# One base for eight tiles of edges and 80 accumulator columns, in place of four tiles and 64 columns, in a graph network of 200,000 edges

## The chip, the cores and the metric

The kernel runs on one core of one Trainium2 chip. The metric is the device time of one execution in microseconds (us); the median of three runs is the time that counts. TensorE is the matmul engine, VectorE and ScalarE the elementwise engines, GpSimd (POOL in the profile) issues the indirect gathers, SyncE (SP) issues plain DMAs.

## What is computed

Four graph layers stand one behind the other, each ahead of it with a layer norm and a residual. Nodes: 12500, with 128 features each. Edges: 200,000, as pairs (src, dst), sorted by dst, so that the edges of one node are neighbours; a node has 16 edges in the mean. All is float32.

```python
def sage(x, src, dst, W, b):                      # layer 0, three times
    agg = segment_sum(x[src], dst, n) * inv[:, None]
    return relu(concatenate([x, agg], -1) @ W + b)

# layer 1: attention over the edges of a node (4 heads of 32), then a feed-forward block
msg = xh[src] * alpha[:, :, None]
out = segment_sum(msg, dst, n)                    # and the sum of alpha beside it

# layer 2: msg = relu(h[src] + edge_attr); aggr = segment_sum(msg, dst, n); two batch norms
# layer 3: x + segment_sum(x[src] + edge_attr, dst, n)
```

What takes the time is `segment_sum(x[src], dst)`: a gather of 200,000 rows of 512 bytes and a sum by sorted destination.

## The kernel before

**Tiles, groups, halves, iterations.** Edges are padded to 98 × 16 tiles of 128 (`TILE`). A tile's rows are gathered into SBUF, one edge in a partition. `GT` = 4 tiles are a group, and 16 tiles (`HALF`) are a half; `GPH` = 16 / `GT` = 4 groups are in a half, `NGRP` = 392 in all. An iteration does two halves, h = 0 and 1; there are `NIT` = 49 iterations.

**The sum by one-hot matmuls.** For each group the smallest dst is its base. `rel_n` holds dst minus base for each edge. VectorE compares it with 0 .. `W` - 1 (`W` = 64) and gets a one-hot matrix of 128 × W for each tile (L803, 16 tiles in one instruction). TensorE multiplies gathered rows and one-hot (L751), and the tiles of a group accumulate in one PSUM bank (`bank_of`), 128 features × W nodes. VectorE then adds the bank to the transposed result `A` at column base (L846); the base is read from SBUF into a register first (L837). If a group spanned W nodes or more, `net.rounds` would be over 1 and the walk would be made again with the window moved by W.

**Stages.** `aggregate` is called six times: agg0, agg1, agg2 (layer 0), agg3 (attention), agg4 (layer 2, `edges`), agg5 (layer 3).

- agg0 also counts edges for each node: VectorE folds the one-hots of a group by L811, and TensorE sums them over the partitions by L756.
- agg0, agg1, agg2 and agg5 are *dense*: as soon as a stretch of 500 nodes is complete (`due`), its dense layer is computed within the same loop, in banks 4 to 7. Their groups have `NB` = 4 banks, the others 8.
- agg3 gathers nothing: its rows were gathered before by `gat_gather` (L1191) and come by plain DMA. A second matmul with 4 weight columns sums the attention weights (L765, 128*4).
- agg4 adds the edge features (loaded by SyncE, L715 to L728) to the rows (L831, VectorE) and applies ScalarE's relu (L661). A second matmul (L765, 128*128) sums the edge features themselves, for agg5. Its edges are dealt to partitions so that a partition's edge features of one group are contiguous: `GT` × 512 bytes.

**Who waits for whom.** Gathers for half h of iteration i + 1 go into the buffer of half h of iteration i, so GpSimd waits for `summed[h]`, which TensorE raises by one for each group (L677); in agg4 it waits for VectorE's `message[h]` (L675). Ahead of each group TensorE waits for `added` (L748), that the add of the group that had the bank is done. VectorE's order in an iteration is written out: stage the index of the next iteration (L162), adds of half 0, compare for half 0 of the next iteration, in agg4 its message too, adds of half 1, dense chunks if due, compare for half 1.

Of the kernel before, what the change touches and what calls it, by code (L numbers as in the profile page):

```python
# [18 lines left out]
I32 = mybir.dt.int32  # L19
# [5 lines left out]
E = 200000  # L25
D = 128
P = 128
# [3 lines left out]
NSUB = N // SUB  # L31
TILE = 128
HALF = 16
GT = 4
GPH = HALF // GT
NHALF = 98
NIT = NHALF // 2
NTILE = NHALF * HALF
NGRP = NTILE // GT
EP = NTILE * TILE  # L40
GE = GT * TILE
W = 64
EPP = EP // P
H = 4
C = D // H
# [53 lines left out]
def allocate(net):  # L99
# [3 lines left out]
    net.work = net.sb("work", [P, 2 * HALF * XW])  # L103
    net.onehot = net.sb("onehot", [P, 2, HALF, W])
    net.src_n = net.sb("src_n", [P, NTILE + 2 * HALF])
# [218 lines left out]
def prepare(net):  # L324
# [6 lines left out]
    nc = net.nc  # L331
    GP = NGRP // GPH
# [7 lines left out]
    src_i = net.B[0:GP, 0:GPH * GE].bitcast(I32)  # L340
    src_f = net.B[0:GP, 2048:2048 + GPH * GE]
    dealt = [net.B[:, 4096 + k * NTILE:4096 + (k + 1) * NTILE] for k in range(2)]
    least, most = net.small[0:GP, 0:GPH], net.small[0:GP, 4:8]
    span = net.small[0:GP, 8:9]
    least_i = net.small[0:GP, 12:16].bitcast(I32)
    row = net.small[0:1, 16:20]
    it_i = net.work[:, 0:W].bitcast(I32)
    zeros = net.C[:, 0:2 * H * NSC // P // 2]
# [3 lines left out]
    lists = [(src_f, net.src_n, False), (rel_f, net.rel_n, False), (src_f, dealt[0], True), (rel_f, dealt[1], True)]  # L352
    tiles = [(fr, to, deal, g, k) for fr, to, deal in lists for g in range(GPH) for k in range(GT)]

    with nc.Block() as block:
# [34 lines left out]
        def _(dve):  # L390
# [59 lines left out]
            for n, (_, to, _, g, k) in enumerate(tiles):  # L450
                dve.wait_ge(turned, n + 1)
                nc.vector.tensor_copy(to[:, 0:NTILE].rearrange("p (a t) -> p a t", t=HALF)[:, :, g * GT + k],
                                      net.psum[:, (n % 2 + 2) * 512:(n % 2 + 2) * 512 + GP]
# [3 lines left out]
        def _(pe):  # L457
# [4 lines left out]
            for n, (fr, _, deal, g, k) in enumerate(tiles):  # L462
                if n >= 2:
                    pe.wait_ge(copied, n - 1)
                group = fr[:, g * GE:(g + 1) * GE]
                tile = (group.rearrange("a (p k) -> a k p", k=GT)[:, k, :] if deal
                        else group[:, k * TILE:(k + 1) * TILE])
# [128 lines left out]
def aggregate(net, tag, table=None, extra=None, follow=None):  # L596
# [10 lines left out]
    nc = net.nc  # L607
# [20 lines left out]

    high = [P, H if attention else P]
    dense = follow and follow.dense  # L630
    NB = 4 if dense else 8
    bank_of = lambda h, q, k: net.psum[0:high[k], (h * SG + q) % NB * 512 + k * W:(h * SG + q) % NB * 512 + (k + 1) * W]
    name = lambda k: [net.sem(f"{tag}_{k}{h}") for h in range(S)]
    index_ready = net.sem(f"{tag}_index")
# [3 lines left out]
    message, attr_loaded, relued = name("message"), name("attr"), name("relued")  # L638
# [6 lines left out]
    with nc.Block() as block:  # L645
# [40 lines left out]
        @block.sync  # L686
        def _(sp):
            if not (attention or edges):
                if dense:
                    follow.sync(sp)  # L690
                return
            if edges:
                sp.dma_start(net.src_n[:, 0:NTILE], net.DEALT[0]).then_inc(lists, 16)
                sp.dma_start(net.rel_n[:, :], net.DEALT[1]).then_inc(lists, 16)
                sp.wait_ge(cleared, 1)
            R = sp.value_load(net.rounds[0:1, 0:1], min_val=1, max_val=256)
            with sp.Fori(0, R) as r:
                with sp.Fori(0, NIT) as i:
                    n = sp.snap(r * NIT + i)
                    for h in range(2):  # L700
                        if attention:

                            sp.wait_ge(message[h], n + 1)
                            sp.dma_start(rows[h], net.G[bass.ds(i * 2 + h, 1), :, :]
                                         .rearrange("a p f -> (a p) f")).then_inc(gathered[h], 16)
                        else:

                            sp.wait_ge(summed[h], n * GPH + GPH)  # L710
                            lane = "(q p k) f -> p q (k f)"
                            slots = attr[h].rearrange("p (q f) -> p q f", q=GPH)
                            edge = net.dram["edge_attr_128"]
                            at = (2 * i + h) * HALF * TILE
                            sp.dma_start(slots[:, 0:2, :], edge[bass.ds(at, 2 * GE), :].rearrange(  # L715
                                lane, q=2, p=P)).then_inc(attr_loaded[h], 16)
                            if h == 0:
                                sp.dma_start(slots[:, 2:4, :], edge[bass.ds(at + 2 * GE, 2 * GE), :].rearrange(
                                    lane, q=2, p=P)).then_inc(attr_loaded[h], 16)
                                continue  # L720
                            with sp.If(i < NIT - 1):
                                more = nc.s_assert_within(at + 2 * GE, 0, E - 2 * GE)
                                sp.dma_start(slots[:, 2:4, :], edge[bass.ds(more, 2 * GE), :].rearrange(
                                    lane, q=2, p=P)).then_inc(attr_loaded[h], 16)
                            with sp.Else():
                                rest = E - (NGRP - 2) * GE
                                sp.dma_start(slots[0:rest // GT, 2, :], edge[E - rest:E, :].rearrange(
                                    "(p k) f -> p (k f)", k=GT)).then_inc(attr_loaded[h], 16)  # L728

        @block.tensor  # L730
# [154 lines left out]
class Shares:  # L885

    dense = False
# [12 lines left out]
class Sage:  # L900
# [6 lines left out]
    dense = True  # L907
# [113 lines left out]
class Project:  # L1021
# [6 lines left out]
    dense = True  # L1028
# [807 lines left out]
class Finish:  # L1836


    dense = True
# [100 lines left out]
```

## Time and profile before

| What | us |
|---|---|
| Runs, median of three (lowest, highest) | 16836.19 (16834.64, 16855.76) |
| Profiled execution, its own time | 16957.4 |
| Profiled execution, span from first to last instruction | 16955.6 |
| GpSimd busy | 9653.8 (57%) |
| TensorE busy, matmul | 6756.4 (40%) |
| VectorE busy | 3233.9 (19%) |
| ScalarE busy | 824.7 (5%) |

The mean granted clock of TensorE is 0.528 of full speed (2.4 GHz), so over most of the span it is the lower of its two levels, 1.2 GHz. Busy shares are means over stages that differ: what an edit is worth is read from its stage. In the rows, POOL is GpSimd, DVE is VectorE, PE is TensorE's matmul and PEld its weight load; L680 is line 680 of the kernel. Idle time stands in brackets in front of the instruction that ends it, with what released it as the profile infers; "remote" and "issue" mean that it names no instruction of this core.

### The profile page before, as it was taken

What the parts mean: (1) busy time and instruction counts of PE and PEld (TensorE: products, weight loads), DVE (VectorE), ACT (ScalarE), POOL (GpSimd) and SP (SyncE); (2) the same over time, 40 slices, a digit from 0 to 9 for tenths busy, and PEclk for the clock granted to TensorE, in tenths of its full rate; (3) what the DMA queues carried; (4) which work ended last, traced back from release to release, by engine and by line L of the source; (5) the groups of instructions that cost most, each with busy time, mean ns of one, the idle gap of its engine ahead of it and who ended that gap; (6) DMA issues with size and microseconds to landing.
All of it is one profiled execution on the core that took longest, in us unless ns stands there. A gap on an engine that the chain in (4) does not pass through costs nothing. (4 is left out here: it accounts for less than half of the span.)

```text
span 16955.6 us, 119259 instructions
## 1 busy us (share of the span) xinstructions
PE 6756.4 (40%) x30243; PEld 5863.6 (35%) x30244; DVE 3233.9 (19%) x6147; ACT 824.7 (5%) x1247; POOL 9653.8 (57%) x9860
## 2 busy tenths in 40 slices
PE   3444443333334444410000009995555555533333
PEld 2333333333333333300000008873555554333333
DVE  3222221000011212200000014444111112311111
ACT  1000000000000000000000000003000000200000
POOL 2666666666666666667777440002666664366666
PEclk8555555555555555555555555557555555655555
DMA  2111111111111221233333212222222222221212
GB/s 87 47 48 47 48 48 45 48 48 48 48 47 53 55 55 54 57 87 100 100 100 99 66 33 87 97 89 84 82 81 80 82 82 89 67 54 52 54 53 53
DMA packets 593155, 1124.64 MB, mean 66 GB/s; under 512 B 220825, under 2 KB 364384, under 8 KB 566578
## 3 DMA queue, kind: packets, MB, share of 16 engines
q0 software_dynamic: 307488, 624.42, 14.6%
q1 hardware_dynamic: 285622, 499.73, 8.8%
q8 instruction: 15, 0.25, 0.0%
q14 instruction: 30, 0.25, 0.0%
HBM read 904.32 MB, written 218.95 MB: 66 GB/s over the span
## 5 line engine op out<-in xcount | busy, mean ns | idle before, releaser
L680 POOL DMA_INDIRECT work<-rows_a,index x4704 | 4587.5, 975 | 2399.1 <-issue 1544.6
L751 PE MATMUL psum<-onehot,work 128*128 128x64 f32 x12544 | 2822.4, 419 | 4459.8 <-DMA work<-rows_a,index 2818.1
L751 PEld LDWEIGHTS psum<-onehot,work 128*128 128x128 f32 x12544 | 2717.3, 328 | 4556.2 <-issue 4424.5
L680 POOL DMA_INDIRECT work<-rows_b,index x3136 | 3118.6, 994 | 1771.6 <-issue 1075.8
L1191 POOL DMA_INDIRECT work<-attention_rows,index x1568 | 1610.9, 1027 | 612.5 <-issue 557.2
L751 PE MATMUL psum<-onehot,regionB 128*128 128x64 f32 x6272 | 1551.9, 416 | 720.1 <-issue 581.2
L751 PEld LDWEIGHTS psum<-onehot,regionB 128*128 128x128 f32 x6272 | 1440.3, 327 | 819.6 <-issue 801.5
L846 DVE TENSOR_TENSOR regionA<-regionA,psum 128x64 f32 x2352 | 508.0, 216 | 5289.9 <-remote 2271.8
L765 PE MATMUL psum<-onehot,regionB 128*4 128x64 f32 (+1 forms) x6272 | 1174.7, 358 | 484.9 <-issue 484.5
L765 PEld LDWEIGHTS psum<-onehot,regionB 128*4 128x4 f32 (+1 forms) x6272 | 1023.8, 223 | 533.3 <-issue 486.8
L182 POOL COPY work<-regionB 128x500 f32 (+1 forms) x75 | 45.5, 606 | 2034.9 <-DVE regionB L561 2034.9
L843 DVE TENSOR_TENSOR regionC<-regionC,psum 128x64 f32 (+1 forms) x1176 | 254.1, 216 | 3594.7 <-remote 2155.8
L1339 PE MATMUL psum<-ident,work 128*128 128x128 f32 x49 | 17.6, 454 | 2214.4 <-POOL work L1294 2214.2
L1339 PEld LDWEIGHTS psum<-ident,work 128*128 128x128 f32 x49 | 8.9, 182 | 2223.1 <-POOL work L1294 2221.4
L803 DVE TENSOR_TENSOR onehot<-rel_n,window 128x1024 f32<-128x1024 f32 x588 | 717.9, 1221 | 244.7 <-issue 225.0
L162 DVE CAST index<-src_n (+1 forms) x301 | 56.0, 187 | 2180.3 <-DMA work<-attention_rows,index 2073.4
L831 DVE TENSOR_TENSOR regionB<-work,regionB 128x2048 f32<-128x2048 f32 x98 | 225.1, 2297 | 449.7 <-DMA regionB<-in_edge_attr 290.0
L661 ACT ACTIVATE regionB<-regionB 128x2048 f32<-128x2048 f32 x98 | 187.2, 1910 | 2402.9 <-DVE regionB L831 1896.4
L756 PE MATMUL psum<-regionC,ones 128*128 128x64 f32 x784 | 246.4, 409 | 88.4 <-issue 87.6
L969 PE MATMUL psum<-regionB,weights 128*128 x100 | 101.5, 1118 | 445.8 <-DVE regionA L959 356.2
L984 ACT ACTIVATE turn<-psum,small 128x500 f32<-128x500 f32 x50 | 33.9, 678 | 4498.1 <-PE psum L970 3033.5
L756 PEld LDWEIGHTS psum<-regionC,ones 128*128 128x128 f32 x784 | 214.2, 328 | 77.7 <-issue 77.7
(253 smaller groups left out, 4471.5 us busy)
## 6 DMA issues: line engine op xcount, KB each, us to landing
gathered_rows<-work SPq DMA_DIRECT2D x98, 1088.0 KB
work<-gathered_rows SPq DMA_DIRECT2D x98, 1088.0 KB, 4.9
regionB<-in_edge_attr SPq DMA_DIRECT2D x195, 512.0 KB
work<-rows_a,index POOLq DMA_INDIRECT x4704
work<-rows_b,index POOLq DMA_INDIRECT x3136
work<-attention_rows,index POOLq DMA_INDIRECT x1568
x_transposed<-regionA SPq DMA_DIRECT2D x75, 250.0 KB, 6.0
rows_a<-regionC SPq DMA_DIRECT2D x50, 250.0 KB
```

What stands on the lines that cost most here:

```text
L162: return net.nc.vector.tensor_copy(net.index[:, :, :].rearrange("p a t -> p (a t)")[:, bass.ds(parity * 2 * HALF, 2 * HALF)], net.src_n[:, ...
L661: nc.scalar.activation(msgs[h], msgs[h], ACT.Relu).then_inc(relued[h], 1)
L680: pool.indirect_dma_start(rows3[h][:, t, :], None, table, bass.IndirectOffsetOnAxis(ap=net.index[:, k, h * ST + t:h * ST + t + 1], axis=0) ...
L751: last = nc.tensor.matmul(bank_of(h, q, 0), msgs3[h][:, t, 0:D], onehot[:, h * ST + t, :], start=(k == 0), stop=(k == GT - 1))
L756: last = nc.tensor.matmul(bank_of(h, q, 1), net.ones[:, :], piles[h][:, q * W:(q + 1) * W], start=True, stop=True)
L765: last = nc.tensor.matmul(bank_of(h, q, 1), lhs, onehot[:, h * ST + t, :], start=(k == 0), stop=(k == GT - 1))
L803: nc.vector.tensor_tensor(onehot[:, h * ST:(h + 1) * ST, :], net.rel_n[:, bass.ds(i * 2 * HALF + h * ST, ST)].unsqueeze(2) .broadcast_to([ ...
L831: nc.vector.tensor_tensor(msgs[h], rows[h], attr[h], ALU.add).then_inc(message[h], 1)
L843: nc.vector.tensor_tensor(Cc[0:high[1], bass.ds(at, W)], Cc[0:high[1], bass.ds(at, W)], bank_of(h, q, 1), ALU.add)
L846: nc.vector.tensor_tensor(A[:, bass.ds(at, W)], A[:, bass.ds(at, W)], bank_of(h, q, 0), ALU.add).then_inc(added, 1)
L969: net.nc.tensor.matmul(dense(net, 0), self.w[:, 0:D], net.col(net.B, c), start=True, stop=False)
L1191: pool.indirect_dma_start(rows3[h][:, t, :], None, net.XH, bass.IndirectOffsetOnAxis(ap=net.index[:, k, h * HALF + t:h * HALF + t + 1], ax ...
```

## The change

A group has eight tiles (1024 edges) in place of four, and its accumulator 80 columns in place of 64. So there are two groups in a half and 196 in all. Everything derived from `GT` and `W` follows: the one-hots are 128 × 80 for each tile, 128x1280 in one compare; a group's matmuls accumulate eight tiles; each half has two reports, two value loads of a base and two adds (of 80 columns) in place of four. The number of edge matmuls stays. `NB` becomes 2 × `GPH` = 4 in all stages; that is an iteration's groups. In agg4 a half's edge features are loaded by one DMA for each group, of the same 512 KB, with contiguous pieces of 4 KB in place of 2 KB.

```diff
-GT = 4
+GT = 8
-W = 64
+W = 80
-    least, most = net.small[0:GP, 0:GPH], net.small[0:GP, 4:8]
+    least, most = net.small[0:GP, 0:GPH], net.small[0:GP, 4:4 + GPH]
-    least_i = net.small[0:GP, 12:16].bitcast(I32)
+    least_i = net.small[0:GP, 12:12 + GPH].bitcast(I32)
-    NB = 4 if dense else 8
+    NB = 2 * GPH
-                            lane = "(q p k) f -> p q (k f)"
-                            sp.dma_start(slots[:, 0:2, :], edge[bass.ds(at, 2 * GE), :].rearrange(
-                                lane, q=2, p=P)).then_inc(attr_loaded[h], 16)
+                            sp.dma_start(slots[:, 0, :], edge[bass.ds(at, GE), :].rearrange(
+                                "(p k) f -> p (k f)", p=P)).then_inc(attr_loaded[h], 16)
                             if h == 0:
-                                sp.dma_start(slots[:, 2:4, :], edge[bass.ds(at + 2 * GE, 2 * GE), :].rearrange(
-                                    lane, q=2, p=P)).then_inc(attr_loaded[h], 16)
+                                sp.dma_start(slots[:, 1, :], edge[bass.ds(at + GE, GE), :].rearrange(
+                                    "(p k) f -> p (k f)", p=P)).then_inc(attr_loaded[h], 16)
...
-                                rest = E - (NGRP - 2) * GE
-                                sp.dma_start(slots[0:rest // GT, 2, :], edge[E - rest:E, :].rearrange(
+                                rest = E - (NGRP - 1) * GE
+                                sp.dma_start(slots[0:rest // GT, 1, :], edge[E - rest:E, :].rearrange(
```

## Rows read from the trace of the kernel before

**Rows 1.** GpSimd's busy time and its gather lines; durations as minimum/median/maximum in ns.
```profile
PE 6756.4 (40%) x30243; PEld 5863.6 (35%) x30244; DVE 3233.9 (19%) x6147; ACT 824.7 (5%) x1247; POOL 9653.8 (57%) x9860
...
L680 POOL DMA_INDIRECT work<-rows_a,index x4704 | 4587.5, 975 | 2399.1 <-issue 1544.6
...
L1191 POOL DMA_INDIRECT work<-attention_rows,index x1568 | 1610.9, 1027 | 612.5 <-issue 557.2
...
L680 POOL DMA_INDIRECT work<-rows_a,index x4704: 942/947/1997, 291.9 to 16930.3; - x196
```

**Rows 2.** Length; PE, PEld, DVE, ACT, POOL busy; clock: agg1, agg3, agg4.
```profile
2620.60:4940.60 2320.00, 814.15 (x3340) 723.28 (x3340) 246.99 (x584) 45.80 (x75) 1536.76 (x1581) 0.51 0.18 48
...
...
10255.20:11370.20 1115.00, 1115.00 (x6265) 984.16 (x6266) 543.32 (x1097) 0.00 (x0) 0.00 (x0) 0.50 0.27 96
11759.40:14279.20 2519.80, 1386.87 (x6138) 1370.42 (x6138) 494.47 (x1009) 185.25 (x97) 1594.10 (x1568) 0.50 0.28 81
```

**Rows 3.** Waits of GpSimd's gathers: total us, times, longest.
```profile
POOL work L680 <- remote: 996.8, 188, 6.7
...
POOL work L680 <- DVE regionB L831: 433.5, 32, 18.2
```

**Rows 4.** Timeline within agg1: start us, length us, engine, line, count, idle time before.
```profile
3992.83 7.09 PE L751 MATMUL psum<-onehot,work 128*128 128x64 f32 x32 [19.37 <-DMA work<-rows_b,index]
...
4006.53 0.22 DVE L846 TENSOR_TENSOR regionA<-regionA,psum 128x64 f32 x1 [11.26 <-remote]
...
4015.71 0.22 DVE L846 TENSOR_TENSOR regionA<-regionA,psum 128x64 f32 x1 [8.96 <-remote]
4016.39 0.95 POOL L680 DMA_INDIRECT work<-rows_b,index  x1 [5.25 <-remote]
4016.72 0.22 DVE L846 TENSOR_TENSOR regionA<-regionA,psum 128x64 f32 x1 [0.79 <-DVE regionA L846]
4017.06 1.23 DVE L803 TENSOR_TENSOR onehot<-rel_n,window 128x1024 f32<-128x1024 f32 x1
4017.65 1.46 POOL L680 DMA_INDIRECT work<-rows_b,index  x1 [0.30 <-issue]
```

**Rows 5.** VectorE's compare, count reduce and message: busy us, mean ns of one.
```profile
L803 DVE TENSOR_TENSOR onehot<-rel_n,window 128x1024 f32<-128x1024 f32 x588 | 717.9, 1221 | 244.7 <-issue 225.0 <-DVE base_now L792 2.9
...
L831 DVE TENSOR_TENSOR regionB<-work,regionB 128x2048 f32<-128x2048 f32 x98 | 225.1, 2297 | 449.7 <-DMA regionB<-in_edge_attr 290.0 <-DMA work<-rows_b,index 151.7 <-issue 8.0
...
L811 DVE TENSOR_REDUCE regionC<-onehot 128x256 f32<-128x1024 f32 x98 | 186.3, 1901 | 3.5 <-issue 0.2
```

**Rows 6.** Timeline within agg1: three transposes of 128 moving columns.
```profile
4028.96 0.84 PE L1001 MATMUL psum<-ident,turn 128*125 128x128 f32 x3
```

**Rows 7.** Timeline within agg3: TensorE's groups, large and small matmuls in turn.
```profile
10604.39 1.02 PE L765 MATMUL psum<-onehot,regionB 128*4 128x64 f32 x8
...
10605.33 1.97 PE L751 MATMUL psum<-onehot,regionB 128*128 128x64 f32 x8
...
10607.23 0.38 PE L765 MATMUL psum<-onehot,regionB 128*4 128x64 f32 x2
```

**Rows 8.** Timeline within agg4: single matmuls, then the end of a pause.
```profile
13081.93 0.27 PE L765 MATMUL psum<-onehot,regionB 128*128 128x64 f32 x1 [2.53 <-issue]
...
13083.33 0.27 PE L765 MATMUL psum<-onehot,regionB 128*128 128x64 f32 x1 [1.14 <-issue]
...
13085.63 0.22 DVE L843 TENSOR_TENSOR regionC<-regionC,psum 128x64 f32 x1 [34.04 <-remote]
...
13086.10 0.39 SPq L715 DMA_DIRECT2D regionB<-in_edge_attr  x1
...
13088.34 1.23 DVE L803 TENSOR_TENSOR onehot<-rel_n,window 128x1024 f32<-128x1024 f32 x1
...
13091.34 2.29 DVE L831 TENSOR_TENSOR regionB<-work,regionB 128x2048 f32<-128x2048 f32 x1 [1.77 <-DMA regionB<-in_edge_attr]
...
13094.45 0.95 POOL L680 DMA_INDIRECT work<-rows_b,index  x1 [14.90 <-DVE regionB L831]
```

More of the change, by code:

```diff
@@ L714, in _ @@
                             at = (2 * i + h) * HALF * TILE
-                            sp.dma_start(slots[:, 0:2, :], edge[bass.ds(at, 2 * GE), :].rearrange(
-                                lane, q=2, p=P)).then_inc(attr_loaded[h], 16)
+                            sp.dma_start(slots[:, 0, :], edge[bass.ds(at, GE), :].rearrange(
+                                "(p k) f -> p (k f)", p=P)).then_inc(attr_loaded[h], 16)
                             if h == 0:
-                                sp.dma_start(slots[:, 2:4, :], edge[bass.ds(at + 2 * GE, 2 * GE), :].rearrange(
-                                    lane, q=2, p=P)).then_inc(attr_loaded[h], 16)
+                                sp.dma_start(slots[:, 1, :], edge[bass.ds(at + GE, GE), :].rearrange(
+                                    "(p k) f -> p (k f)", p=P)).then_inc(attr_loaded[h], 16)
                                 continue
                             with sp.If(i < NIT - 1):
-                                more = nc.s_assert_within(at + 2 * GE, 0, E - 2 * GE)
-                                sp.dma_start(slots[:, 2:4, :], edge[bass.ds(more, 2 * GE), :].rearrange(
-                                    lane, q=2, p=P)).then_inc(attr_loaded[h], 16)
+                                more = nc.s_assert_within(at + GE, 0, E - GE)
+                                sp.dma_start(slots[:, 1, :], edge[bass.ds(more, GE), :].rearrange(
+                                    "(p k) f -> p (k f)", p=P)).then_inc(attr_loaded[h], 16)
                             with sp.Else():
-                                rest = E - (NGRP - 2) * GE
-                                sp.dma_start(slots[0:rest // GT, 2, :], edge[E - rest:E, :].rearrange(
+                                rest = E - (NGRP - 1) * GE
+                                sp.dma_start(slots[0:rest // GT, 1, :], edge[E - rest:E, :].rearrange(
                                     "(p k) f -> p (k f)", k=GT)).then_inc(attr_loaded[h], 16)
```

## The prediction

> **What bounds the kernel now.** I read the page first. GpSimd is busy 57% of the span, no engine more, and nearly all of it is gathers, one indirect DMA for 128 edges: 7840 of L680 and 1568 of L1191 [rows 1]. Then the stretches of the stages that walk over the edges, three of which stand in [rows 2]. In those that gather, GpSimd is by far the busiest engine or (agg4) level with TensorE; TensorE is busy all the time in one alone, the attention sum (10255 to 11370), which gathers nothing. So two bounds: the GpSimd chain in agg0, agg1, agg2, agg4 and agg5, TensorE in agg3.
>
> The timeline of one iteration of agg1 shows how the GpSimd chain is built [rows 4]. A gather takes 0.95 us and the next starts 0.30 us behind it, 1.25 us each, so 32 gathers are 40.0 us. An iteration takes 2320.0 / 49 = 47.3 us [rows 2], the start of the stage included (46.5 in the steady part). The difference has two parts. One is a pause of 5.25 us ahead of the gather at 4016.39: it refills the buffer of half 0 and must wait until TensorE has reported the last group of that half (`summed[0]`). The whole run has 188 such waits, 996.8 us [rows 3]. The report is late, not the matmuls: half 0's 32 matmuls are recorded from 3992.83 to 3999.92, yet VectorE adds its second group at 4006.53 and its third at 4015.71, 4 to 5 us after GpSimd stopped. I don't know what holds the reports back; I only see that they come through when the gathers stop. The other part is collisions: the gather that starts at 4017.65, under VectorE's one-hot compare, takes 1.46 us and not 0.95. All gathers of that kind together have a median of 947 ns and a mean of 975 [rows 1]: 28 ns × 1568 = 44 us in each stage, 0.45 us for each of its 98 compares.
>
> **The change part by part.**
>
> Matmuls, 64 to 80 columns. In steady state a 128x128 matmul of 64 columns takes (7.09 - 0.42) / 31 = 0.215 us, the last one's recorded 0.42 us aside [rows 4]. One of 128 columns takes (0.84 - 0.42) / 2 = 0.21 us at the same clock [rows 6]. The pace is therefore set by something that 64 and 128 columns share (both load 125 or 128 weight columns), and 80 lies between them: 0. This covers L751, L756 and the edge matmuls of L765. Not so the attention's small matmuls with 4 weight columns: eight of them with 64 columns take 1.02 us, a pace of about 0.107 [rows 7], and by columns it becomes 0.133. A group of four tiles in agg3 takes 10607.23 - 10604.39 = 2.84 us: 8 × 0.107 for the small ones, 8 × 0.2135 for the large ones, and 0.28 for the two changes between the shapes. Two old groups are 5.69 us. A new group of eight tiles is 16 × 0.2135 + 16 × 0.133 + 0.28 = 5.83. So +0.14 us × 196 groups = **+27 us**, all on the path, as TensorE never rests there. Ends: +84 if the changes of shape cost nothing less often (3136 × 0.027), -55 if the small ones don't grow at all (196 × 0.28).
>
> Compare, L803, from 1024 to 1280 elements. 1024 take 1.22 us and 2048 (L831, the same kind of instruction) 2.30 [rows 5], 1.05 ns an element: 1.49 us, +0.27. VectorE has room for it (247 of 2320 us busy in agg1 [rows 2]), so by itself it costs nothing; through the gathers it does. A gather that starts during a compare ends about 0.81 us after the compare's end: 4017.65 + 1.46 is 0.82 after 4018.29 [rows 4]. It is held until the compare is over. A compare that is 0.27 longer thus holds GpSimd 0.27 longer where it already held it, and the row of the mean says that nearly every compare does. That is the lower end: 0.27 × 98 × 4 = 106 us in the four gathering stages beside agg4, 92 if one compare in eight falls where no gather is due.
>
> The add, L846, from four groups in a half to two. Two of four adds go; each takes 0.22 us and starts 0.8 to 1.0 us behind the one before it, and the compare stands behind the last. What the adds give back is VectorE time that nobody waits for. But the compare moves. Before, the late report let VectorE add the third group at 4015.71, the fourth at 4016.72 and compare at 4017.06. Now the last group's add is the one at 4015.71; the compare runs from 4016.05 to 4017.54. GpSimd restarts at 4016.39 as before, and its first gather is held: to 4017.54 + 0.81 = 18.35, 1.96 us and not 0.95 (the longest gather of before took 1997 ns [rows 1]). The second one is free of it. So +1.01 - 0.51 = +0.50 us, 0.23 more than from the length alone. The compare of half 1 also comes earlier, at random against the gathers: between +0.27 and +0.50. Upper end: 1.0 us × 49 × 4 = 196 us. Between 92 and 196 I take **+125 us**, since in agg0 and agg2 the work after the adds (reduce, dense chunk) already shifts the compare away from the restart.
>
> The Trainium skill, "SBUF — State Buffer", section "Who interferes with whom", says that a VectorE instruction with two SBUF inputs contends with a GpSimd instruction that reads SBUF, and that whoever is second waits for the whole instruction; one with a PSUM input doesn't count. By that rule the adds taken away give the gathers nothing and the compare made longer costs them all of its length; the trace agrees (1.46 us under L803, 0.95 under the L846 at 4016.72).
>
> Counts in agg0. The reduce L811 (1.90 us for 1024 elements [rows 5]) grows to about 2.4 us 98 times, the count matmul halves. The reduce stands behind the compare, TensorE needs it some 20 us later: 0. If it held gathers as the compare does, +0.47 × 98 = +46 us.
>
> Banks and waits. With two groups in a half, four banks hold two halves, so in dense stages a matmul no longer waits for the add of the half before. That wait fell on half 1, whose result GpSimd wants some 20 us later: 0. Nothing is queued behind new waits.
>
> The edge stage, agg4. Its pauses are longer: 433.5 us until L831 [rows 3]. In the one shown, VectorE gets the reports at 13085.63, adds groups 1.12 us apart, compares at 13088.34 and then still waits 1.77 us for the edge load that was issued at 13086.10; L831 starts at 13091.34 and GpSimd 3.1 us later [rows 8]. Adds saved (2 × 1.1) and compare grown (0.27) both vanish behind the load. The load moves the same bytes with half as many pieces, 4 KB instead of 2 KB; no row has a 4 KB piece. It took 13091.34 - 13086.10 = 5.2 us; I bound it between nothing and 1 us less, 0 to -49 us, and set it against the compares that hold gathers here (0.27 × 98 = +26): **0**, ends -50 and +60.
>
> Preparation: 64 transposes and copies as before, bases in one row of 196: 0. SyncE's and ACT's queues issue what they did.
>
> The pause itself. TensorE runs the same matmuls in each half; only its reports are half as many. I keep the pause at its length; what speaks against that is a rival.
>
> Sum: 27 + 125 + 0 = +152 us. The profiled execution goes from a span of 16955.6 (16957.4 with what lies around it) to 17109. The median of the runs is 0.7% below it; the same sum on it gives 16836 + 152 = **16988 us**, say 16990.
>
> **The rivals.**
>
> Faster: the pause shrinks. The reports come through one at a time while gathers run (second group 4006.53, third 4015.71, that is 9 to 11 us apart), and half as many might all be through before GpSimd needs the last one. For: those distances. Against: in agg4, while gathers run, single matmuls follow each other 1.4 us apart (13081.93, 13083.33), the engine idle 2.53 and 1.14 us ahead of them [rows 8], so the price looks like one for each matmul, and these stay as many; and the third and fourth group are added 1.0 us apart, so they are let through together when gathers stop. Price: 996.8 us of pauses; half gone is -500, with +152 it gives 16490. It decides from 0.8 us off each of the 188 pauses (152 / 188), from where the sum turns negative.
>
> No change: what the compare takes from a gather is given back by the pause, since the pause ends at a fixed moment of TensorE and not so long after the last gather. Then only agg3 is left, 16863. For: the pause is a wait. Against: the reports are released by GpSimd's stopping.
>
> Slower, more: with sixteen matmuls to a report the first one is late as well, and VectorE gets both at the restart; pauses grow by 1 us: +196 + 152, 17185.
>
> The change doesn't do what it says: if eight tiles spanned 80 nodes anywhere, `rounds` would be 2 and each aggregation would run twice, about 29,000 us. The drawn destinations span at most 71 in any 1024 edges, 37 in any 512, so one round in both.
>
> **How the numbers follow.** Forecast 0.57 (all slower); pause shrinks 0.24 (nearly all faster, the smallest gains within 0.2%); given back 0.12 (within 0.2%, which is 34 us and about what a measurement can tell from no change); pause grows 0.06; two rounds 0.01. Faster 0.23, same 0.14, slower 0.63. The likeliest case alone runs from 16836 + 92 - 55 - 50 = 16823 to 16836 + 196 + 84 + 60 + 46 = 17222. The range reaches down to a pause shortened by somewhat over two fifths, 16550, and up to 17230.
>
> **What would show it.** L803 at 1.49 us, x588; L846 x1176. L680 with a mean near 990 and not 975, a median still 947. TensorE's L751 at the same mean of 419. agg3 27 us longer. The 188 waits at 5.3 us each. If their sum falls below 850 us, my step on the pause is wrong and the kernel is faster; if L680's mean stays, the step on the held gather is.

## The result and the profile after

The kernel with eight tiles to a group and 80 columns takes **16440.10 us** (median of 4 runs, 16433.56 to 16445.67) beside 16840.03 us of the kernel before on the same chip (16834.64 to 16855.76). The ratio is 0.977, 95% interval 0.9758 to 0.9782: 400 us faster, where 150 us slower was forecast, and below the range of 16550 to 17230. Unchanged on another chip it gave 0.9744 (0.9728 to 0.976).

The profiled execution spans 16443.0 us. Lines of the page, groups and the wait that answer to [rows 1], [rows 5] and [rows 3] (line numbers of the kernel after are one lower from L751 on):

```profile
PE 6230.6 (38%) x29851; PEld 5397.4 (33%) x29852; DVE 3125.4 (19%) x4383; ACT 824.4 (5%) x1247; POOL 9777.0 (59%) x9860
...
PEclk8555555555555555555555556986555556655555
```

```profile
L680 POOL DMA_INDIRECT work<-rows_a,index x4704 | 4663.9, 991 | 2270.4 <-issue 1540.1
L802 DVE TENSOR_TENSOR onehot<-rel_n,window 128x1280 f32<-128x1280 f32 x588 | 874.9, 1488 | 226.7 <-issue 216.1 <-DVE base_now L791 3.0
```
```profile
L845 DVE TENSOR_TENSOR regionA<-regionA,psum 128x80 f32 x1176 | 273.2, 232 | 5257.0 <-remote 2816.2 <-PE psum L750 1408.5 <-DMA running_max<-regionC 700.6
```
```profile
POOL work L680 <- remote: 737.9, 150, 6.2
```

GpSimd is busy longer, not shorter (9777 us, before 9654): its gathers still collide, and more. The digit row is the news: TensorE's granted clock, 5 tenths in most of the run, shows 6, 9 and 8 where agg3 lies. The windows of agg1, agg3 and agg4 (length, busy time of PE, PEld, DVE, ACT, POOL, clock, DMA share, GB/s) say how much that is, against [rows 2]:

```profile
2618.30:4902.30 2284.00, 814.12 (x3336) 725.22 (x3336) 221.33 (x374) 45.73 (x75) 1556.61 (x1569) 0.51 0.18 48
10205.00:10959.20 754.20, 678.34 (x6272) 627.13 (x6272) 511.37 (x705) 0.00 (x0) 0.00 (x0) 0.90 0.40 142
11343.90:13781.80 2437.90, 1394.64 (x6098) 1354.91 (x6098) 456.22 (x623) 183.32 (x96) 1611.02 (x1568) 0.50 0.28 83
```

agg3, the one stage that TensorE bounds, fell from 1116 us at a clock of 0.50 to 754 us at 0.90: 362 of the 400 us. The timeline of its start shows the level change (start, length, engine, line, count; the trace holds two records for each matmul, so x16 is eight tiles and the x8 of [rows 7] four, and what the prediction counts as 32 matmuls of a half are the records of 16):

```profile
10204.95 3.70 PE L750 MATMUL psum<-onehot,regionB 128*128 128x80 f32 x16 [12.04 <-DVE regionB L824]
10208.58 2.30 PE L764 MATMUL psum<-onehot,regionB 128*4 128x80 f32 x16
10210.81 3.70 PE L750 MATMUL psum<-onehot,regionB 128*128 128x80 f32 x16
10214.44 2.06 PE L764 MATMUL psum<-onehot,regionB 128*4 128x80 f32 x16
10216.44 2.01 PE L750 MATMUL psum<-onehot,regionB 128*128 128x80 f32 x16
10218.38 1.27 PE L764 MATMUL psum<-onehot,regionB 128*4 128x80 f32 x16
10219.58 2.01 PE L750 MATMUL psum<-onehot,regionB 128*128 128x80 f32 x16
```

At 1.2 GHz a group takes 10210.81 - 10204.95 = 5.86 us, within 0.03 of the 5.83 that was forecast. From 10216.44 on, at 2.4 GHz, it takes 3.14 us (10216.44 to 10219.58). 196 groups of 3.14 are 615 us; the rest of the 754 is 76 us in which TensorE waits (754.2 - 678.3) and 63 us that the groups at the low level take beyond 3.14 each. The waits are 24 of about 3.1 us, for VectorE's L824 (such as the one that ends at 10244.92), and each of the 24 later stretches at the low level begins during one or shortly behind it; with the first stretch they last 144 us.

### The profile page after: what moved, and what is told of

The parts are those of the page before. It is cut to its first block and busy times, and to the rows that moved or that the text cites. A ratio compares the mean times of both kernels' runs of the same rounds, so it can differ in the third digit from the quotient of the medians.

```text
span 16443.0 us, 107327 instructions
## 1 busy us (share of the span) xinstructions
PE 6230.6 (38%) x29851; PEld 5397.4 (33%) x29852; DVE 3125.4 (19%) x4383; ACT 824.4 (5%) x1247; POOL 9777.0 (59%) x9860
## 5 line engine op out<-in xcount | busy, mean ns | idle before, releaser
L680 POOL DMA_INDIRECT work<-rows_a,index x4704 | 4663.9, 991 | 2270.4 <-issue 1540.1
L750 PE MATMUL psum<-onehot,work 128*128 128x80 f32 x12544 | 2762.0, 418 | 4410.6 <-DMA work<-rows_a,index 3032.2
L680 POOL DMA_INDIRECT work<-rows_b,index x3136 | 3167.2, 1010 | 1618.4 <-issue 1073.4
L750 PE MATMUL psum<-onehot,regionB 128*128 128x80 f32 x6272 | 1177.6, 353 | 730.9 <-issue 462.0
L750 PEld LDWEIGHTS psum<-onehot,regionB 128*128 128x128 f32 x6272 | 1112.0, 267 | 790.7 <-issue 751.8
L845 DVE TENSOR_TENSOR regionA<-regionA,psum 128x80 f32 x1176 | 273.2, 232 | 5257.0 <-remote 2816.2
L764 PE MATMUL psum<-onehot,regionB 128*4 128x80 f32 (+1 forms) x6272 | 1024.1, 329 | 461.6 <-issue 461.3
L764 PEld LDWEIGHTS psum<-onehot,regionB 128*4 128x4 f32 (+1 forms) x6272 | 946.3, 210 | 493.0 <-issue 474.5
L802 DVE TENSOR_TENSOR onehot<-rel_n,window 128x1280 f32<-128x1280 f32 x588 | 874.9, 1488 | 226.7 <-issue 216.1
L842 DVE TENSOR_TENSOR regionC<-regionC,psum 128x80 f32 (+1 forms) x588 | 136.4, 232 | 3172.0 <-remote 2103.0
L810 DVE TENSOR_REDUCE regionC<-onehot 128x160 f32<-128x1280 f32 x98 | 225.2, 2298 | 3.3
```

The costliest lines, as they stand in the source:

```text
L680: pool.indirect_dma_start(rows3[h][:, t, :], None, table, bass.IndirectOffsetOnAxis(ap=net.index[:, k, h * ST + t:h * ST + t + 1], axis=0) ...
L750: last = nc.tensor.matmul(bank_of(h, q, 0), msgs3[h][:, t, 0:D], onehot[:, h * ST + t, :], start=(k == 0), stop=(k == GT - 1))
L764: last = nc.tensor.matmul(bank_of(h, q, 1), lhs, onehot[:, h * ST + t, :], start=(k == 0), stop=(k == GT - 1))
L802: nc.vector.tensor_tensor(onehot[:, h * ST:(h + 1) * ST, :], net.rel_n[:, bass.ds(i * 2 * HALF + h * ST, ST)].unsqueeze(2) .broadcast_to([ ...
L810: nc.vector.tensor_reduce(piles[h].rearrange("p (q w) -> p q w", w=W), onehot[:, h * ST:(h + 1) * ST, :].rearrange("p (q k) w -> p q w k", ...
L842: nc.vector.tensor_tensor(Cc[0:high[1], bass.ds(at, W)], Cc[0:high[1], bass.ds(at, W)], bank_of(h, q, 1), ALU.add)
```

## The experiments

Times of the runs on agg3, each against the kernel before on its own chip at its own time, and agg3 in each profile. "Tiles in a row" is how many tiles' matmuls of one shape (128 or 4 weight columns) follow each other on TensorE in agg3.

| kernel | tiles in a row, columns | time | ratio (95%) | agg3, clock |
|---|---|---|---|---|
| before, again | 4, 64 | 16834.8 | 1.0003 (0.9993-1.0014) | 1116.0, 0.50 |
| gt4_halfreports | 4, 64 | 16828.3 | 1.0000 (0.9987-1.0014) | 1116.0, 0.50 |
| gt4_w72 | 4, 72 | 16885.0 | 1.0028 (1.0016-1.0040) | 1163.0, 0.50 |
| after_runs8 | 4, 80 | 16913.2 | 1.0045 (1.0028-1.0062) | 1210.0, 0.50 |
| gt8_w64 | 8, 64 | 16727.9 | 0.9942 (0.9920-0.9965) | 1059.8, 0.50 |
| gt4_w72_runs16 | 8, 72 | 16584.0 | 0.9852 (0.9835-0.9869) | 844.2, 0.88 |
| gt8_w72 | 8, 72 | 16444.8 | 0.9771 (0.9749-0.9792) | 773.4, 0.85 |
| after | 8, 80 | 16440.1 | 0.9770 (0.9758-0.9782) | 754.2, 0.90 |
| gt4_w64_runs32 | 16, 64 | 16839.7 | 0.9951 (0.9935-0.9966) | 1023.1, 0.73 |
| gt8_w72_runs32 | 16, 72 | 16639.4 | 0.9834 (0.9816-0.9852) | 872.9, 0.81 |

### Which part of the change brings the clock

**gt8_w64**: eight tiles, 64 columns as before. Edges that lie 64 or more above their group's base are left out of the sums, and one round is forced (in `...`).

```
-W = 80
+W = 64
...
```


> The changed kernel with the window taken back from 80 to 64 columns, one round forced: edges whose destination lies 64 or more above their group's base are left out of the sums. Theory A (columns): what lets TensorE run at 2.4 GHz in the attention sum agg3 is the wider moving operand; with 64 columns the clock stays at 1.2 GHz there, agg3 takes 1090 to 1116 us as before, and the whole is about 16440 + 340 = 16780 us, less some 60 for shorter compares, 16720. Theory B (groups): it is the longer runs of one shape (16 and 16 matmuls in place of 8 and 8); then agg3 stays near 750 us and the whole is 16340 to 16400. On the pauses: if they shrank because of fewer reports and adds, the waits of GpSimd's gathers stay at or below 740 us in total; the collisions fall back from a mean gather of 0.99 to 0.975 us.

**gt8_w72**: `W = 72` in the kernel after. The widest group spans 71, so nothing is left out.

> The changed kernel with 72 columns in place of 80 (the widest group spans 71 nodes above its base, so that nothing is left out). Theory A (columns): the clock of agg3 is between: either as high as with 80 (agg3 near 750 us, the whole 16400) or as low as before (agg3 near 1110, the whole 16750). Theory B (groups): agg3 near 750 us, the whole 16400 us. In both the compare is 1.36 us and the mean gather 0.983.

**gt4_w72**: `W = 72` in the kernel before.

> The kernel before with 72 columns in place of 64, still four tiles in a group. Theory A (columns): if 72 are enough, the clock of agg3 rises here too, agg3 near 750 to 800 us and the whole about 16500; Theory B (groups): agg3 stays at 1.2 GHz and takes 1116 + 3136 x 0.013 = 1157 us, the whole is 16840 + 41 + about 60 for longer compares = 16940 us. The pauses stay at 188 and 1000 us.

**gt4_halfreports**: the kernel before, with one report of TensorE for two groups.

```
-                            last.then_inc(summed[h], 1)
+                            if q % 2:
+                                last.then_inc(summed[h], 2)
```


> The kernel before, but TensorE reports two groups at once (a semaphore increment of 2 behind every second group); matmuls, adds, banks and compares stay. If the number of reports sets the pauses, GpSimd's waits fall from 997 us to the 738 us of the changed kernel or below, and the whole to about 16600; if it is the adds, or the banks that a matmul waits for, they stay at 950 to 1050 us and the whole within 50 us of 16840. agg3's clock should stay low.

Their windows of agg3, in this order without the last:

```profile
10184.00:11243.80 1059.80, 1059.75 (x6272) 994.15 (x6272) 481.17 (x705) 0.00 (x0) 0.00 (x0) 0.50 0.29 101
```
```profile
10205.80:10979.20 773.40, 696.32 (x6272) 648.55 (x6272) 495.04 (x705) 0.00 (x0) 0.00 (x0) 0.85 0.39 138
```
```profile
10215.30:11378.30 1163.00, 1162.96 (x6272) 1016.19 (x6272) 562.75 (x1097) 0.00 (x0) 0.00 (x0) 0.50 0.26 92
```

Neither part alone brings the clock. Both give my low-level terms back: eight tiles alone -56 us (I had 196 × 0.28 = 55), eight more columns alone +47 (3136 × 0.0133 = 42). TensorE is busy all of the 1060 and 1163 us, and still at 1.2 GHz. Reports half as many leave the time as it was (1.000). GpSimd's remote waits at L680 fell to 788.9 us in 175, which neither answer had (738 or less, or 950 to 1050); before_again, the unchanged kernel, has 888.8 in 175. Whatever its label, idle time over 1.5 us between gathers is 1112 us in agg0, agg1, agg2 and agg5 together, where three profiles of the unchanged kernel have 1158 to 1232. So fewer reports may shorten the pauses somewhat, but the half that my faster rival priced at 500 us does not go, and the kernel gains nothing.

**gt4_w72_runs16** and **after_runs8** change the order on TensorE in agg3: the one gives the kernel of four tiles (72 columns) the run length of eight tiles, the other gives the kernel after the run length of four. The first reports two groups at once; in the second the small sums also get banks of their own (not shown below).

```
+                            if attention:
+                                if q % 2 == 0:
+                                    continue
+                                for b, cols in ((0, slice(0, D)), (1, slice(D, D + H))):
+                                    for t in range((q - 1) * GT, (q + 1) * GT):
+                                        last = nc.tensor.matmul(bank_of(h, t // GT, b), ...)
+                                last.then_inc(summed[h], 2)
+                                continue
```
```
+                            if attention:
+                                for k0 in range(0, GT, 4):
+                                    for b, cols in ((0, slice(0, D)), (1, slice(D, D + H))):
+                                        for k in range(k0, k0 + 4):
+                                            last = nc.tensor.matmul(...)
+                                last.then_inc(summed[h], 1)
+                                continue
```


> Four tiles to a group and 72 columns, and in agg3 alone the order on TensorE is changed: the 16 matmuls of 128 rows... of 128 columns of weights for two groups and then the 16 of 4 columns for both, where it was 8 and 8 (one report for both groups). Theory A (the clock is granted by how long runs of one kind of matmul are, or by how densely TensorE streams without a change of shape): agg3 rises to 2.4 GHz as in the eight-tile kernels, takes 760 to 850 us in place of 1163, and the kernel 16480 to 16560. Theory B (the run length is not it; what eight tiles bring is something else, as fewer banks opened or fewer reads by VectorE): the clock stays at 0.50, agg3 takes 1163 less 49 to 60 for the shape changes saved, about 1108, and the kernel comes out near 16830.

> The kernel after (eight tiles, 80 columns), with the order of four tiles on TensorE in agg3 alone: 8 large... four large matmuls, four small, four large, four small, in one group's accumulators (the small ones in a bank of their own), so that shapes change as often as in the kernel before. Theory A (run length decides the clock): agg3 falls back to 1.2 GHz, takes about 1116 + 84 = 1200 us where it took 754, and the kernel takes 16440 + 445 = 16885, slower than before. Theory B (the run length is not it): the clock stays near 0.90, agg3 takes 754 plus some 30 for the shape changes at the high level, and the kernel 16470.

Windows of agg3, the first and then the second:

```profile
10214.80:11059.00 844.20, 678.17 (x6272) 629.60 (x6272) 562.29 (x1095) 0.00 (x0) 0.00 (x0) 0.88 0.36 127
```
```profile
10209.80:11419.80 1210.00, 1210.00 (x6272) 1042.32 (x6272) 515.57 (x705) 0.00 (x0) 0.00 (x0) 0.50 0.25 88
```

Theory A holds in both directions. The kernel after, with its matmuls in fours, loses the high clock and the whole gain (1210 us in agg3, 1.0045); the four-tile kernel in eights gets it (0.88; 844 us lie within the 760 to 850 expected, the kernel's 16584 is 24 above its range). What is left between 844 and 754 is waiting: TensorE is idle for 844.2 - 678.2 = 166 us, mostly for VectorE's adds, of which there are twice as many.

**gt4_w64_runs32** and **gt8_w72_runs32**: the same edit with all 16 tiles of a half in a row (`if q < SG - 1: continue`, `range(0, SG * GT)`), in the kernel before and in the kernel after with 72 columns.

> The kernel before (four tiles, 64 columns), with one change in agg3 on TensorE: the large matmuls of all 16 tiles of a half-iteration, then the small ones of all 16, reported together; so runs of one kind are four times as long as in before and twice as long as in the kernel of eight tiles and 64 columns, which stayed at a granted clock of 0.50. Theory A (only the length of the runs counts, and 64 columns need a longer run than 72 do): agg3 rises to 2.4 GHz, takes 760 to 860 us, and the kernel 16500 to 16590. Theory B (64 columns never get the high level in this pattern, however long the run; the accumulator's width is the second condition by itself): the clock stays at 0.50, agg3 takes 1116 less 1.5 times 56 or 1032, plus what TensorE now waits for the adds, and the kernel 16750 to 16830.

> Eight tiles and 72 columns, with agg3's large matmuls of both groups of a half-iteration first (16 tiles) and then the small ones of 16 tiles. The same kernel in runs of 8 tiles took 773 us in agg3 at a mean clock of 0.85, with single stretches at the low level in between. Theory A (a longer run holds the high level more firmly): the mean clock rises to 0.93 or more, agg3 takes 720 to 755 us and the kernel 16390 to 16430. Theory B (the level drops whenever TensorE has waited, and a report for 16 tiles at once makes it wait for VectorE's adds, as the four-tile kernel in runs of 8 tiles waited 178 us there): agg3 takes 780 to 860 us and the kernel 16450 to 16530.

```profile
10250.00:11273.10 1023.10, 782.18 (x6272) 755.38 (x6272) 546.45 (x1091) 0.00 (x0) 0.00 (x0) 0.73 0.30 105
```
```profile
10248.40:11121.30 872.90, 728.04 (x6272) 701.15 (x6272) 496.81 (x703) 0.00 (x0) 0.00 (x0) 0.81 0.35 123
```

The first falls between my two theories: 64 columns do reach the high level when the run is 16 tiles long, so 72 is no condition by itself, but only for part of the time, and one report for 16 tiles leaves TensorE idle for 241 us. The second goes theory B's way, somewhat past its 860 us: the mean clock falls from 0.85 to 0.81, TensorE waits 145 us where it waited 77, and the kernel is slower than with runs of eight. Both the run of one shape and the columns thus bear on the clock, as kernels compared here; why they do stays open. A longer run is no gain once a report comes too late for VectorE.

### The collisions, and what gives them back

**after_window_psum** and, unchanged, **window_psum_again**: the kernel after, with the compare's list of column numbers in PSUM in all aggregations but agg2.

```
+    window = net.window[:, :] if isinstance(follow, Project) else net.psum[:, 5 * 512:5 * 512 + W]
...
-            nc.vector.tensor_copy(net.window[:, :], net.window0[:, :])
+            nc.vector.tensor_copy(window, net.window0[:, :])
...
-                        net.window[:, :].unsqueeze(1).broadcast_to([P, ST, W]),
+                        window.unsqueeze(1).broadcast_to([P, ST, W]),
```


> The kernel after, with the list of column numbers that the comparison reads (the window) held in PSUM in every aggregation but the third, so that the comparison reads one operand from SBUF in place of two. In the kernel after a gather that begins under the comparison takes 1.46 us in place of 0.95, and the gathers of the dense stages carry 292 us more than at 0.945 us each, 292 against 224 at 64 columns. Theory A (the gathers suffer from the comparison's two SBUF inputs, and what they lose is on the path): the gathers' excess falls by 60 to 150 us over agg0, agg1 and agg5, and the kernel by 60 to 120, to 16320 to 16380. Theory B (the excess falls, but the pauses before the gathers grow by most of it, since both end with the same messages; as from 80 to 64 columns, where 68 us less excess came with 50 us more pauses): the kernel takes 16400 to 16440. Theory C (the length of the comparison alone counts, not where its operands lie): nothing moves, or reading PSUM makes the comparison slower than 1.49 us and the kernel 16450.

**before_again** and **before_third** are the kernel before, and **after_again** the kernel after, unchanged.

> The kernel before, unchanged, for a second profiled execution: the first one spans 16956 us, some 115 above the median of its runs, and its agg2 took 2341 us where three other four-tile kernels took 2277 to 2326. If that excess lies in single pauses of that one execution, this profile spans 16840 to 16900, its ratio is 1.000, agg3 takes 1116 us at a granted clock of 0.50 again, and agg4 comes out near 2486 as in the two other four-tile kernels, so that about 35 us of the 82 that agg4 seemed to lose by the change are the first profile's own. If the excess belongs to the kernel, agg2 is 2341 and agg4 2520 again.

> The kernel before, unchanged, as a partner for the runs beside it. In the last two experiments the kernel before took 15479 us on that occasion, where it had taken 16770 to 16950 on all others, and the traces taken there show hardly any waits of GpSimd for a late report. Theory A (the late reports come from outside the kernel and are there or not for a whole occasion): this profile has either some 170 to 190 such waits and 890 to 1000 us of them, with a time near 16840, or next to none, with a time near 15480, and nothing in between. Theory B (the two last experiments themselves took the waits away and the time of 15479 has another reason): the waits stand in this profile whatever its time.

> The kernel after, unchanged. With late reports: ratio 0.977 again, as collisions are given back by shorter pauses. Without late reports there is no pause that could give them back, and the sum of the prediction without its wrong step should hold: agg3 -362, collisions +92 to +125 over agg0, agg1, agg2 and agg5, so 15479 - 250 = about 15230, ratio 0.984 (0.982 to 0.986). The rival is that collisions cost nothing there either: 15479 - 362 = 15117, ratio 0.977.

> The kernel after with the window in PSUM in all aggregations but the third, unchanged from its first run. With late reports: the time of the kernel after, within 0.1%, as before. Without late reports the collisions it takes away are on the path: it is faster than the kernel after by 150 to 230 us (the excess of the gathers, 226 us in the three stages), so near 15030, ratio 0.970. The rival (a gather's excess doesn't count) gives the time of the kernel after in either case.

after_window_psum took 16519.5 us (0.9767, 0.9747 to 0.9786), before_again 16834.8 (1.0003). before_third, after_again and window_psum_again ran on one chip: 16908.9 (1.0006), 16488.5 (0.9744) and 16503.3 us (0.9752, 0.9736 to 0.9768). Over agg0, agg1, agg2 and agg5 I added up, from each trace, what the gathers take beyond 0.945 us each, and the pauses over 1.5 us between them:

| agg0 + agg1 + agg2 + agg5 | before_third | after_again | window_psum_again |
|---|---|---|---|
| gathers beyond 0.945 us | 170 | 302 | 94 |
| pauses over 1.5 us | 1201 | 1065 | 1248 |
| time of the four stages | 9135 | 9148 | 9109 |

Gather lines and GpSimd's waits of after_again and then of window_psum_again:

```profile
L680 POOL DMA_INDIRECT work<-rows_a,index x4704 | 4674.1, 994 | 2287.7 <-issue 1538.0 <-remote 560.9 <-DMA running_max<-regionC 113.0
...
POOL work L680 <- remote: 787.8, 153, 6.6
```
```profile
L681 POOL DMA_INDIRECT work<-rows_a,index x4704 | 4533.1, 964 | 2402.8 <-issue 1552.9 <-remote 730.2 <-PE psum L751 58.6
...
L803 DVE TENSOR_TENSOR onehot<-rel_n,psum 128x1280 f32<-128x1280 f32 x490 | 726.0, 1482 | 175.8 <-issue 164.8 <-DVE base_now L792 2.9
...
POOL work L681 <- remote: 1017.4, 184, 7.0
```

The collisions are real: the change adds 132 us of them (agg0 45, agg1 33, agg2 28, agg5 26; the first profiles of the two kernels differ by 108), and a compare that reads one operand from PSUM, as long as the other (1482 ns against 1489), takes 208 us away. Neither moves the four stages' time by more than 0.5%: the pauses take 136 us less in the one case and 183 us more in the other. In agg0 of after_window_psum the starts of the halves are most often 20.0 and 26.1 us apart, 46.1 together; in before_again most often 20.4 and 25.7, and 46.1 or 46.2 together in 28 of 48 iterations. It is no constant: the medians of unchanged kernels lie between 46.0 and 46.7, and in agg1 of the kernel after the iterations spread evenly over 44.6 to 48.0. Theory B holds. The Trainium skill, "SBUF — State Buffer", section "Who interferes with whom", says that a VectorE instruction with at most one SBUF input, outside the modes that use two ports, does not contend with GpSimd; the traces agree (gathers at 964 ns in place of 994, and only in the stages so changed).

**after_halfrows**: in agg0, agg1, agg2 and agg5 each gather fetches 64 numbers in place of 128, and the buffer is cleared first. **after_halfmatmuls** and, unchanged, **halfmatmuls_again**: in those stages the scatter matmul of every second tile is left out.

```
-                            for k in range(GT):
+                            step = 1 if attention or edges else 2
+                            for k in range(0, GT, step):
```


> The kernel after, but in agg0, agg1, agg2 and agg5 each gather fetches 64 of the 128 numbers of a row (as many rows, half the bytes; what is computed there is therefore not the reference's, and a clearing of the buffer adds some 4 us to each stage). The window in PSUM took nearly all of the collisions from the gathers, 226 us over the three dense stages, and the pauses ahead of them grew by 218, so an iteration kept its 46.0 us: something ends at a fixed time after the restart that is neither GpSimd's gathers nor the comparison. Theory A (it is the transfer of the gathered bytes): the pause shrinks, its 52 to 58 in a stage and 233 to 257 us fall by more than a half, agg1 takes 2000 to 2120 us in place of 2254. Theory B (it is something for each gather or each row, not for the byte): the pauses stay within 15 us, agg1 takes 2240 to 2265.

> The kernel after, but in agg0, agg1, agg2 and agg5 TensorE makes the scatter matmul of every second tile only (the others' edges are left out of the sums). Theory A (the pause is set by TensorE's own work, its matmuls creep while the gathers run and its report comes late for that reason, whatever the recorded times say): half the matmuls end that much sooner, the pauses of a stage fall from about 240 us to under 120, agg1 takes under 2140 us. Theory B (the report is late whatever TensorE has to do, it waits for something on GpSimd's side or on the way): pauses and stages stay within 15 us, agg1 takes 2240 to 2265.

> The kernel after with every second scatter matmul of agg0, agg1, agg2 and agg5 left out, unchanged from its first run, which fell on the occasion without late reports and so could not answer. With late reports: theory A (TensorE creeps through its matmuls while the gathers run, each held for itself) has the pauses of a stage at under 120 us in place of about 240, agg1 at under 2140 us; theory B (the report is late whatever TensorE has to do) has pauses within 15 us of the kernel after's. Without late reports: no pause in either, and the time is that of the kernel after less 0 to 120 us.

The first two answer neither question. On that occasion the kernel before took 15479 us (15476 to 15480), 8% less than on all others, on a chip that had given 16825 earlier; this is a condition outside the kernel. after_halfrows and after_halfmatmuls took 15233 us (0.9842, 0.9813 to 0.987) and 15113 us (0.9764, 0.9735 to 0.9792). In the trace of the second, GpSimd at L680 waits for TensorE 100 times, 44 us in all and never over 2.1 us; the rest is the issue time between gathers. Gaps over 1.5 us are 114 us in the four stages.

```profile
4007.67 3.70 PE L751 MATMUL psum<-onehot,work 128*128 128x80 f32 x16 [18.27 <-DMA work<-rows_b,index]
...
4009.89 0.24 DVE L846 TENSOR_TENSOR regionA<-regionA,psum 128x80 f32 x1 [18.50 <-PE psum L751]
```

VectorE adds a group 2.2 us after its matmuls begin, with gathers running. Here the report is not late, hardly a pause is left (27 us in agg1, where the kernel after had 233), and agg1 takes 2050 us in place of 2254. The same program, run again as halfmatmuls_again, met the late reports. So the late report of [rows 4] is not settled by the program; it is there on some occasions (all others of this study) and not on one.

agg3 takes 754 us in both traces, 362 off, and after_halfmatmuls is 366 us faster than the kernel before beside it, although its gathers take 271 us beyond 0.945 each in the four stages. By my expectation of +92 to +125 for collisions where no pause gives them back, it should have gained less. No trace of the kernel before exists from that occasion, nor the whole kernel after, so what collisions cost without pauses stays open.

halfmatmuls_again met the late reports and took 16678.9 us, 0.9856 (0.984 to 0.9872): slower than the kernel after, with less to do. agg0, agg1 and agg5 take 2284, 2244 and 2239 us, with pauses of 233, 235 and 228 (after_again 262, 250 and 251). Half the matmuls thus take 15 to 29 us of 250 from the pauses, not half of them, so theory A falls, and theory B (within 15 us) holds only roughly; in agg2, beside the dense work, pauses went from 302 to 576 us, which neither theory had and which I can't explain.

### agg4

**after_halflines**: each of agg4's edge transfers as two of half the line (2 KB as before the change in place of 4 KB; in the expectation the lines are called 1 and 2 KB, which is half of what they are).

```
+                            HL = GT // 2 * D
+                            def halves(q, start):
+                                for j in range(2):
+                                    sp.dma_start(slots[:, q, j * HL:(j + 1) * HL], ...)
```


> The kernel after, with each transfer of edge features in agg4 made as two of half the line: 1 KB to a partition at a time as in the kernel before, where the change made it 2 KB. Theory A (agg4's 50 to 80 us come from the halved number of DMA packets, 25000 fewer, beside which the gathers run): agg4 goes back from 2438 to about 2487 us and the kernel to 16490. Theory B (they come from fewer and longer groups on TensorE and half as many adds on VectorE): agg4 stays at 2430 to 2445, and the ratio to before stays 0.977.

It took 16455.0 us, 0.9774 (0.9758 to 0.979), and agg4 2445 us: theory A falls. Kernels with four tiles took 2474 to 2520 us in agg4, those with eight and the compare in SBUF 2430 to 2473 (2500 in gt8_w72_runs32); on one chip, before_third 2505 and after_again 2464. So about 40 us of the gain are agg4's. The line length alone doesn't bring them. With the window in PSUM agg4 takes 2530 and 2510; what sets it stays open.

## Why the prediction was wrong, step by step

- **agg3, +27: wrong in sign and size, -362.** The step that failed is an assumption that I did not write down: that the matmuls of agg3 keep the clock of [rows 2] and [rows 7]. At that clock the arithmetic held (group 5.86 us against 5.83; -56 and +47 against -55 and +42 for the two parts, run singly). I read the granted clock of 0.50 as a fixed rate of the stage, in which TensorE was busy without a break, and had no rival for it. What the runs showed in its place: the clock follows the order of the matmuls, and the mean granted clock of 0.90 in place of 0.50 makes the stage 362 us shorter. The Trainium skill, "TensorE: Matmul & The Clock Gate", Part 1, says that activity releases the gate; by that page alone the stage of [rows 2], busy for all of its 1115 us, should already have stood at 2.4 GHz. The trace disagrees. That disagreement was in view before the change, and was the sign that the level of this stage could move.
- **Compares holding gathers, +125: the size was right, its place on the path was not.** 132 us more on the gathers (before_third to after_again), 108 in the first profiles. I had expected less in agg0 and agg2 than in the others; agg0 has the most. Their sum is taken off the pauses (-136). My "given back" rival, at 0.12, names the mechanism; its reason, a pause that ends at a moment not tied to the last gather, fits the 46 us that an iteration keeps. Shown is that pauses and collisions replace each other; what fixes the length of an iteration is not.
- **The pause itself, kept at 5.3 us: wrong as a step.** 996.8 us in 188 waits became 737.9 in 150, below the 850 that I had named. Part of that is the label: waits put down to the DMA running_max<-regionC rose from 27.0 us (5) to 109.8 (24), and the unchanged before_again has only 888.8 remote. All gaps over 1.5 us in the four stages went from 1232 us (1158 in before_again) to 1036. That brings no time: halfreports, at 788.9 us of remote waits, gives 1.000, so my sign "below 850, then the kernel is faster" was none.
- **Compare, adds, reduce**: L802 1488 ns (forecast 1.49 us), 1176 adds, L810 2298 ns (I had 2.4 us). L680 means 991 ns, and 1010 on its second line (forecast near 990).
- **agg4, 0 (-50 to +60)**: about -40, within the bounds, cause open.
- **The sum.** before_third to after_again: span 16893.6 to 16492.6, -401. agg3 -364, agg4 -41, the four gathering stages +13, the rest -9. With the clock as it was, after_runs8 shows what my sum amounts to: 16913, +71 us, of which agg3 is +94: my upper end of +84 was the case of as many changes of shape as before, which is this kernel's.

The faster outcome had 0.23, all of it on shorter pauses, which came and brought nothing; that the kernel did get faster owes nothing to that reason. The range missed because no term allowed for a change of clock.

## What to carry to other kernels

Read the granted clock of every stage that TensorE bounds as a quantity that the order of its matmuls can change: 0.50 beside a busy share of 100% is a lead, and matmuls with few weight columns that alternate with full ones are the first thing to regroup. Here that order alone, at eight tiles and 80 columns, lies between 1.0045 and 0.9770 of the kernel before. At the low level the parts of the change are small: eight tiles alone gave 98 us (56 of them in agg3), while the whole change with runs of four tiles cost 71. And before pricing a collision on an engine that also pauses, ask what ends the pause: where it is not the engine's own last instruction, as seems the case here, the pause can pay for the collision.

## What the runs showed of the hardware that was not expected

- TensorE busy for 1210.00 us of 1210.00 stays at 1.2 GHz when four tiles of one shape alternate with four of the other; with eight in a row and 72 or 80 columns it stands at 2.4 GHz for most of the stage (mean 0.85 to 0.90).
- In the kernel after, each of the 24 later stretches at 1.2 GHz in agg3 begins during one of TensorE's 24 waits of about 3.1 us or shortly behind it.
- The same program, on the same chip at another time, ran 8% faster (15479 and 16825 us), and the two traces of that time, of changed kernels, have TensorE's reports mostly on time: a time of this kernel only compares with one taken beside it.
